# A two-layer graph kernel with the first rows in a new order: small loads behind x, last unit rows on GpSimd, E transposes between loads, one low part of x on VectorE

## What is computed

```python
deg = jnp.clip(adj.sum(axis=1), 1.0)
dis = deg ** (-0.5)
diffusion = (dis[:, None] * adj * dis[None, :]) @ x - x
norms = jnp.maximum(jnp.linalg.norm(x, axis=-1), 1e-8)
sim = x @ x.T / (norms[:, None] * norms[None, :])
attn = softmax(beta * sim * adj, axis=1)
x = layernorm(x + diffusion + sigmoid(alpha) * (attn @ x - x))
x = layernorm(x + relu(adj @ (x @ weights)))
```

## Time and profile before

| | before |
|---|---|
| median of three runs | 679.48 us |
| the profiled execution, its own time | 679.01 us |
| its span | 677.2 us |
| TensorE busy | 652.0 us, 96% of the span |
| VectorE, ScalarE, GpSimd busy | 561.9, 436.2, 245.5 us |
| DMA | 105.30 MB, mean 155 GB/s |

### The profile page before, as it was taken

The page is one execution under the profiler, slowest core; times in us unless marked ns, Lnnn a source line. Parts: engine busy times, 40 slices in busy tenths (PEclk is TensorE's granted clock), DMA queues, the critical chain, the costliest instruction groups (busy, mean ns, idle before and its releaser), DMA issues.

```text
span 677.2 us, 17913 instructions
## 1 busy us (share of the span) xinstructions
PE 652.0 (96%) x5623; PEld 517.4 (76%) x5623; DVE 561.9 (83%) x1678; ACT 436.2 (64%) x885; POOL 245.5 (36%) x229
## 2 busy tenths in 40 slices
PE   6679999999999999999999999899999999999997
PEld 6347777777777777777777776799888888888886
DVE  4879999999999999999999999767767766666664
ACT  5989998998999999989999988512222223111111
POOL 2899446455455464454464557300000000000000
PEclk8999999999999999999999999999999999999999
DMA  6589999999999999999999994300000000000000
GB/s 252 187 222 237 256 264 239 256 255 237 263 257 248 250 255 251 247 266 248 254 247 256 261 234 81 67 1 1 0 0 0 0 0 1 17 15 31 15 15 31
DMA packets 154538, 105.30 MB, mean 155 GB/s; under 512 B 135696, under 2 KB 136208, under 8 KB 154512
## 3 DMA queue, kind: packets, MB, share of 16 engines
q1 hardware_dynamic: 154080, 104.94, 61.1%
q10 hardware_dynamic: 432, 0.07, 0.1%
HBM read 69.34 MB, written 2.10 MB: 105 GB/s over the span
## 4 chain that ended last, share of the span: by engine, by line
PE 85%; DVE 5%; DMA 3%; POOL 3%; ACT 2%; SPq 1%; issue 1%; ACTq 0%; DVEq 0%; POOLq 0%
PE ps_e L1111 31%; PE ps_s L981 21%; PE ps_e L1013 8%; PE ps_e L992 7%; PE ps_acc L1013 7%; PE ps_e L1016 4%; PE ps_acc L1016 3%; DMA eTx<-e_parts 2%; DVE e_parts L717 2%; DMA col<-in_L_gnn_beta 1%; PE ps_e L1030 1%; DVE scores L696 1%; PE ps_at L965 1%; POOL x_parts L341 1%; PE ps_s L1030 1%
## 5 line engine op out<-in xcount | busy, mean ns | idle before, releaser
L981 PE MATMUL ps_s<-xn_parts,xn_signed 128*128 128x512 f16 x756 | 203.7, 379 | 5.5 <-DVE cmax L696 5.5
L696 DVE CUSTOM_DVE_ANT_1 scores<-ps_s,adj_bytes 128x512 f32<-128x512 f32 x252 | 171.4, 682 | 16.9 <-PE ps_s L981 9.3
L502 ACT ACTIVATE scores<-scores,col 128x1024 f32<-128x1024 f32 x128 | 157.4, 1232 | 4.5 <-DVE col L707 4.3
L326 POOL TENSOR_SCALAR e_parts<-scores 128x1024 f16<-128x1024 f32 x64 | 80.4, 1256 | 157.3 <-ACT scores L502 84.7
L448 ACT ACTIVATE adj_bytes<-land 128x1024 uint8<-128x1024 f32 x128 | 133.5, 1047 | 1.6 <-POOL packed L318 1.6
L1111 PE MATMUL ps_e<-x_parts,stage 128*128 128x256 f16 x1024 | 113.0, 273 | 0.0
L1111 PEld LDWEIGHTS ps_e<-x_parts,stage 128*128 128x128 fp8e4 x1024 | 100.2, 98 | 11.5
L1111 PE MATMUL ps_e<-y_parts,stage 128*128 128x256 f16 x896 | 105.4, 273 | 0.2
L981 PEld LDWEIGHTS ps_s<-xn_parts,xn_signed 128*128 128x128 f16 x756 | 69.5, 98 | 41.7 <-DVE cmax L696 5.5
L717 DVE SCALAR_TENSOR_TENSOR e_parts<-scores,e_parts 128x1024 f16<-128x1024 f32 x64 | 97.5, 1524 | 0.5 <-POOL e_parts L326 0.4
L509 ACT ACTIVATE eT_parts<-ps_e 128x512 f16<-128x512 f32 x128 | 75.7, 591 | 32.0 <-PE ps_e L992 31.4
(11 more groups left out here) (132 smaller groups left out, 992.2 us busy)
## 6 DMA issues: line engine op xcount, KB each, us to landing
land<-in_adj SPq DMA_DIRECT2D x128, 512.0 KB, 4.7
x_keep<-in_x SPq DMA_DIRECT2D x4, 512.0 KB, 8.6
out<-u SPq DMA_DIRECT2D x7, 256.0 KB, 2.0
eTx<-e_parts SPq DMA_TRANSPOSE x64, 5.1
out<-u SPq DMA_DIRECT2D x1, 192.0 KB, 1.9
eT_parts<-in_L_gnn_weights ACTq DMA_DIRECT2D x1, 64.0 KB, 8.7
scores<-in_L_gnn_weights SPq DMA_DIRECT2D x1, 64.0 KB, 2.5
out<-u SPq DMA_DIRECT2D x1, 64.0 KB, 1.6
```

Source lines behind the costliest of these rows:

```text
L326: nc.gpsimd.tensor_scalar(e_parts[:, n, 0, :], scores[:, q, (n + 2) * CH:(n + 3) * CH], E_SCALE, 1.0, ALU.mult, ALU.mult).wait_op(sign_don ...
L502: nc.scalar.activation(piece, piece, ACT.Exp, bias=neg_max[q], scale=abs_beta, accum_out=csum[:, q, i:i + 1]).then_inc(exp_done, 1)
L696: nc.vector.tensor_tensor_reduce(scores[:, q, o:o + BANK].rearrange("p (k q) -> p k q", k=K), score_bank(h, r == 0 if start else False).re ...
L981: ins = nc.tensor.matmul(score_bank(h, start), xn_signed[:, q, part, :], xn_parts[:, other, o:o + BANK], start=(part == 0 and other == 0), ...
```

## The change

Only the order and the place of work in the first rows change; every operation on data stays, but one piece of x no longer goes through `x_scale` and GpSimd's subtraction. It is split by one VectorE instruction instead.

- SyncE issues the three small loads, behind x and ahead of the first `adj` pieces. ScalarE issues none.
- `unit_rows(3)` runs on GpSimd between its two first `sign_block`s, in place of `unit_half` on ScalarE.
- VectorE does `norms2(0)` first. The two waits on small loads move behind `norms2(3)` and `rnorm(3)`. The first two `mask`s go ahead of `xnt_low(6)`, and `x_low(3)` comes in front of `ex_low(1, 1, 0)`.
- GpSimd: `x_split(1)` moves behind the first two `ex_high`s, and the fourth split keeps only its high part.
- SyncE: `turn_ex(0, 0, 0)` moves ahead of the last two pieces of adj row 2, `turn_ex(0, 0, 1)` ahead of the first two of row 3.
- ScalarE: `e_high(0, 0)` moves ahead of the last exponential and cast. TensorE's `keep_busy` counts change (2 becomes 3 and 4), and `turn_rows(5)` and the second `cosines` move up.

```diff
+            sp.dma_start(alpha_c, alpha.rearrange("(a o) -> a o", o=1).to_broadcast([P, 1])).then_inc(small_loaded, 16)
+            sp.dma_start(beta_c, beta.rearrange("(a o) -> a o", o=1).to_broadcast([P, 1])).then_inc(small_loaded, 16)
+            sp.dma_start(wts_early, weights).then_inc(w_loaded, 16)
...
-                    if k == K - 1 and i == 1:
-                        turn_ex(0, 0, 1)
+                    if k == K - 2 and i == 1:
+                        turn_ex(0, 0, 0)
                 if k == K - 2:
-                    turn_ex(0, 0, 0)
+                    turn_ex(0, 0, 1)
...
+            unit_rows(3)
             sign_block(1, 1, first=True)
             pool.wait_ge(scales_done, 1)
             x_split(0)
-            x_split(1)
             pack(0, 0, first=True)
             ex_high(0, 0, 0, first=True)
             ex_high(0, 0, 1, first=True)
+            x_split(1)
             sign_block(2, 0)
             x_split(2)
-            x_split(3)
+            x_high(3)
...
-            turned_high(1)
-            unit_half(3, 0)
-            turned_high(2)
-            unit_half(3, 1)
-            turned_high(3)
+            for g in range(1, 4):
+                turned_high(g)
...
             cast(1, 1, 2, first=True)
+            e_high(0, 0, True)
             exps(0, 0, 1)
...
+            def x_low(n):
+                q = X_ORDER[n]
+                dve.wait_ge(x_hi, n + 1)
+                nc.vector.scalar_tensor_tensor(x_parts[:, q * TC:(q + 1) * TC, D:2 * D], x_keep[:, q * TC:(q + 1) * TC, :],
+                                               x_up, x_parts[:, q * TC:(q + 1) * TC, 0:D],
+                                               ALU.mult, ALU.subtract).then_inc(x_lo, 1)
...
+                    if start and h == 7:
+                        x_low(C - 1)
                     if h == 7:
                         ex_low(r + 1, 1 - q, 0)
...
-            for g in range(4):
-                turn_rows(g)
+            turn_rows(0)
+            turn_rows(1)
+            keep_busy(3)
+            turn_rows(2)
+            turn_rows(3)
             pe.wait_ge(great_done, 1)
             nc.tensor.transpose(ps_at[0:2, 0:P], great, ident[:, :]).then_inc(great_turned, 1)
-            keep_busy(2)
+            keep_busy(4)
             turn_rows(4)
+            turn_rows(5)
             pe.wait_ge(great_diag, 1)
...
-            turn_rows(5)
             cosines(0, 0, 0, start=True)
+            cosines(0, 0, 1, start=True)
             turn_rows(6)
-            cosines(0, 0, 1, start=True)
```

More of the change, by code:

```diff
@@ L332, in x_scale, with x_high @@
                                         ALU.mult, ALU.mult).then_inc(x_scaled, 1)
+            def x_high(n):
+                q = X_ORDER[n]
+                nc.gpsimd.tensor_scalar(x_parts[:, q * TC:(q + 1) * TC, 0:D], x_keep[:, q * TC:(q + 1) * TC, :], x_up, 1.0,
+                                        ALU.mult, ALU.mult).then_inc(x_hi, 1)
             def x_split(n):
@@ L460, in turned_high @@
                                      ACT.Copy).then_inc(xnt_hi, 1)
[L462 to L469, removed]
             squares(0)
@@ L514, in row @@
                 for h in range(H):
-                    if h % 2 == 0:
+                    if h % 2 == 0 and not (start and h == 0):
                         e_high(r, h // 2, start)
@@ L642, in unit_rows @@
                     ALU.mult).then_inc(xn_done[q], 1)
+            norms2(0)
+            norms2(1)
+            rnorm(0)
+            rnorm(1)
+            unit_rows(0)
+            norms2(2)
+            norms2(3)
+            dve.wait_ge(small_loaded, 32)
+            link(nc.vector.tensor_scalar(sign_beta, beta_c, 0.0, 2.0, ALU.is_ge, ALU.mult))
+            link(nc.vector.tensor_scalar(sign_beta, sign_beta, -1.0, None, ALU.add))
+            nc.vector.tensor_scalar(abs_beta, beta_c, sign_beta, None, ALU.mult).then_inc(sign_done, 1)
+            rnorm(2)
+            rnorm(3)
+            dve.wait_ge(w_loaded, 16)
+            link(nc.vector.tensor_reduce(great[:, 1:2], wts_early, AX.X, ALU.max, apply_absolute_value=True))
+            nc.vector.tensor_reduce(great[:, 0:1], norm[:, :], AX.X, ALU.max).then_inc(great_done, 1)
             def xnt_low(g):
@@ L701, in mask, with store_adj @@
                 ).wait_op(sign_done, 1, "sem-ge").then_inc(scores_done, 1)
+            xnt_low(0)
+            xnt_low(1)
+            xnt_low(2)
+            dve.wait_ge(great_turned, 1)
+            link(nc.vector.tensor_reduce(top[0:2, :], ps_at[0:2, 0:P], AX.X, ALU.max))
+            nc.vector.tensor_scalar(pow2[0:2, :], ident[0:2, 0:2], top[0:2, :], None,
+                                    ALU.mult).then_inc(great_diag, 1)
+            xnt_low(3)
+            dve.wait_ge(great_spread, 1)
+            link(nc.vector.tensor_scalar(pow2, ps_at[:, 2 * P:2 * P + 2], 1e-30, 1e30, ALU.max, ALU.min))
+            link(nc.vector.tensor_scalar(pow2.bitcast(I32), pow2.bitcast(I32), 0x7F800000, None, ALU.bitwise_and))
+            link(nc.vector.reciprocal(rpow2, pow2))
+            nc.vector.tensor_scalar(x_up, rpow2[:, 0:1], X_SCALE / XN_SCALE, None, ALU.mult).then_inc(scales_done, 1)
+            xnt_low(4)
+            xnt_low(5)
+            mask(0, 0, 0, start=True)
+            mask(0, 0, 1, start=True)
+            xnt_low(6)
+            xnt_low(7)
+            for h in range(2, H):
+                mask(0, 0, h, start=True)
+            def store_adj(r):
+                dve.wait_ge(adj_turned, r + 1)
+                nc.vector.tensor_copy(packT[:, r, :], ps_at[:, 0:CH // K].bitcast(U32)).then_inc(adj_stored, 1)
             def row_max(r, q):
@@ L743, in total_step @@
                 ins.then_inc(total_done, 1)
-            for h in range(H):
-                mask(0, 0, h, start=True)
             row_max(0, 0)
```

43 lines of the change are left out of this document (3 added, 40 removed).

## The result

The changed kernel takes 678.43 us (median of 20 runs), the kernel before 679.49 us (median of 20). The ratio is 0.9985, with a 95% interval of 0.9979 to 0.9992: about 1.0 us faster, 0.15%. I had called a difference under 0.3% not measurable; the interval leaves out 1, so this one is measured. One run of the changed kernel (761.8 us) and one of the kernel before (854.98 us) were far slower than the rest, and the ratio leaves them out. The profiled execution spans 676.4 us, before 677.2. The forecast was 676.8 us with a shift of 2.7. The time lies inside the range (674.8 to 680.5), but the range is 5.7 us wide and holds "no change" too. The likeliest case, a gain above 2.0 us, did not happen, and less than half of the 2.7 us came.

A forecast was written before the change was run, and what follows sets the result against it. It took the first rows' chain (beta load, VectorE, then GpSimd's list) as the bound, TensorE alone in the loops. Gains less waits left a 2.7 us shift: 679.01 - 2.7 = 676.3 profiled, 676.8 median, range 674.8 to 680.5.

The forecast's parts named there:

- The likeliest case: Whole kernel: a 2.7 us shift giving a 676.8 us median; chance 0.47, of which 0.07 below the 2.0 us bound.
- What bounds the kernel: First rows against loops: TensorE alone counts from 100 to 400 us, so an earlier start there is kept to the end.
- Small loads behind x: Start: small loads hold up x; with x in front its first piece lands at 4.9 us, where squares started at 7.00.
- VectorE up to the row maximum: First row: low parts start at 13.3 us, the maximum at 24.6 to 24.8 against 29.73, 4.9 us sooner.
- Exponentials and transposes: After the maximum: first transpose issued 8 us sooner, but 3.0 us of waits for adj pieces; 2.9 of 4.9 us given back.
- Second row: Row 1: `x_low` takes 1.6 us, packing is turned at 47.8 and the DMA transposes used at 54.0, a 2.7 us shift.
- The sum: Whole kernel: 679.01 - 2.7 = 676.3 us for the profiled execution, 676.8 for the median.
- x slow for itself: Start: first DMAs are slow whatever runs beside them, x lands as before; 679 to 680.5 us, chance 0.17.
- Pieces not held: Adj row 2: pieces take 3.7 and 4.2 us as alone, ScalarE waits 1.5 us less; 675.3 us, chance 0.09.
- Small loads slow behind x: Start: weights land at 17.8 us and VectorE waits ahead of every low part; 2.2 us loss, 681.7 us, chance 0.12.
- Second-row prices: Row 1: `x_low` takes 2.06 us and a transpose 5.6 to 7; shift 1 to 1.5, 678.2 us, chance 0.15.
- Two of my own signs of being wrong: Listed beforehand as showing the forecast wrong: `x_low` waiting for GpSimd, and TensorE waiting in the loops; no size given.

The follow-up runs named there:

- the one with the scaling on ScalarE: Changed kernel with VectorE's scaling of a 2x2 block made by ScalarE instead: 677.33 us against 678.80 for the kernel before, ratio 0.9976.
- the one with `x_low` in the gap: Kernel before with small loads moved behind x, plus `x_low` on VectorE two masks earlier than the change has it: 676.73 us against 679.15, ratio 0.9977.
- the loads alone: Kernel before with only the small loads and VectorE's two waits for them moved: 677.16 us against 678.80; again, 676.82 against 679.15.
- the old turn order: Changed kernel with the first two DMA transposes issued where the kernel before did: 678.11 us against 679.25 for the kernel before, ratio 0.9987.
- the filler run: Kernel before with three spare TensorE matmuls added at the start of row 1: 678.55 us against 678.80 without them, ratio 1.0002.
- undone one way: Changed kernel with the unit rows of x's last piece made on ScalarE again, in two halves: 677.81 us against 679.25 for the kernel before, ratio 0.9988.

## Why the prediction was right or wrong

- **What bounds the kernel: half right.** The first rows do decide, and the stretch from 100 us on is closed in every run. But "that shift is kept to the end" failed. From row 2 to row 7 the changed kernel loses 0.9 us, the one with the scaling on ScalarE 1.4, the one with `x_low` in the gap 1.9; the loads alone 0.3 to 0.5, the old turn order nothing. Where a loss can be put to an instruction, it is a wait for a DMA transpose between 53 and 88 us. These waits, behind row 2's maximum, go with the losses: 0.77 us for 0.9 in the changed kernel, 1.04 for 1.4 with the scaling on ScalarE, 1.70 for 1.9 in the gap, 0.44 and 0.56 for 0.3 and 0.5 with the loads alone, none in the old turn order. The kernel before has none either, except in the filler run, where x came early: 0.57 for 1.2. In the loops the DMA engines have a share of 1.00 beside TensorE's 299.88 of 300, and I read that row for TensorE alone. That the two end nearly together I take from these waits. Why one kernel loses 1.9 us and another none stays open; no run changed the load on the DMA engines alone.
- **Small loads behind x: right.** x's first pieces at 4.0 and 5.3 for a forecast of 4.9 and 6.2, and the first transpose at 10.80 for 10.4, clock 1.00. The third and fourth piece came at 8.3 and 9.6 for 7.5 and 8.8. This step carries the whole gain: 1.7 and 1.6 us alone, by ratios of 0.9975 and 0.9976. But "in one ring they need no turns with x" is not the whole of it: from 8.0 to 8.8 us, 51 of 74 packets are small and the rate is 59 GB/s.
- **VectorE up to the row maximum: "Unit rows 3 go to GpSimd into a stretch where it waits for the scales" failed.** It is true of GpSimd and cost VectorE 1.57 us (1.97 for 0.40), on the path of the scales. The low parts start at 13.56 for 13.3, the maximum at 26.31 for 24.6 to 24.8. This term is the largest part of the difference: with the scaling on ScalarE the maximum came 1.27 us sooner, 0.29 of that because the low parts started sooner, and 0.6 us of the block was still there.
- **Exponentials and transposes: right mechanism, term too large.** First transpose issued at 31.67 for 29.6, later by the above. The waits for adj pieces are 1.77 us for 3.0: both landed 4.4 to 4.9 us from issue, and the queue was held for 2.17 us where I took 3.34 from the earlier trace rows. Third `e_high` at 40.86 for 40.2.
- **Second row: right to 0.8 us, then wrong.** `x_low` took 1.65 us for 1.6 and ended at 47.7 for 47.1, but that size was right by luck: 1.26 of its own and the rest behind GpSimd, which I had ruled out by the rows. `ex_low` behind it took 2.05 for 1.3, so row 1's transpose was issued at 49.76 for 48.4; TensorE did not wait for it. TensorE turned the packing at 48.51 for 47.8 and reached row 1's transposes at 54.83 for 54.0, so the shift there was 1.9. But I counted only what was on its way to that point. TensorE, late by its wait for `x_low`, released ScalarE's `e_high` and casts late (a 1.31 us wait at 50.69), and VectorE's masks behind these held TensorE for 0.48 at 54.18. At row 2 the shift is 1.5. A loss of 1.0 to 1.7 us from row 1 to row 2 is in every run with `x_low` at that place, and in neither run of the loads alone.
- **The sum.** 2.7 us forecast, less 0.8 up to 54 us, less 0.4 to row 2, less about 0.6 in the loop, is 0.9, and the spans differ by 0.8. The sum was made one shift at a time; the gain of the loads and the price of the other parts (1.5 us by the two runs side by side) were never set apart. Of this price `x_low`'s place may explain 0.6 to 0.9, by runs in the kernel with the loads alone; in the changed kernel itself `x_low` was not moved into the gap. The port block explains 0.6 to 1.6 at the first exponentials, but what of it reaches the end is open: undone one way it gave 0.9988, the other 0.9976, against the changed kernel's 0.9985 and 0.9993. The places of `x_split(1)`, `e_high(0, 0)`, the two first masks and `keep_busy` had no run of their own, so how the price divides stays open.

**The rivals.** x slow for itself: fallen. Pieces not held: they were held, by less. Small loads slow behind x: they take 7.2 to 7.6 us and beta is there when VectorE asks for it at 12.5, so this has fallen. Second-row prices, 678.2 us: nearest in time, but by another cause, since neither cost what it says: `x_low` took 1.65 us, and the third transpose landed in 4.3. Two of my own signs of being wrong came true beside the right ones, `x_low` waiting for GpSimd and TensorE waiting in the loops, and both name places where some of the 2.7 us went. One slip in the range: a loss can be measured above 681.5, not above 680.5, which is only where a rival ends.

## What to carry to other kernels

A change of many parts is to be priced part by part and run part by part: here one part gave 1.6 to 1.7 us, and the others took some 40 to 70% of it back (side by side 1.5 of 2.3 us by the medians, 1.2 of 1.6 by the ratios) while most of them looked free. When work goes to an idle engine, ask not only whether that engine has time but which instructions of the engine that shares its port run beside it, the smallest ones above all if they stand on the path. And look for a gap of the other engine, ahead of the place that waits, for work that moves there: between the two places of `x_low` lay 1.8 us at row 2, though only 0.5 to 1.0 in the whole time, with overlapping intervals. An early gain is worth no more than what the DMA queue behind it can follow.

## What I had not expected of the hardware

- A VectorE instruction on 2x2 elements took 1.97 us beside a 1.90 us GpSimd instruction, and 0.22 to 0.40 where only the end of one was beside it. It ended 0.02 us behind the other in all of these but the shortest. The price of such a block is about the other's remaining time, whatever the size of the blocked one.
- Three loads of 128 runs each (two of 4 bytes, one of 512), on a second queue, brought x's load from 405 to 113 GB/s and its first piece from 4.0 to 6.8 us. Behind x in one queue they took 7.2 to 7.6 us. x's third piece came 0.8 us later than forecast there, while small packets held the rate at 59 GB/s, and its arrival spread over 1.7 us from run to run; that they held it up is my reading, no run took them out.
